# Fetching the features' operand pair by pair, with norm rows from short sends, in a linear-attention and expert kernel

## The reference

```python
def _phi(x, omega):
    m = omega.shape[1]
    proj = jnp.einsum('bhtd,dm->bhtm', x, omega)
    norm_sq_half = 0.5 * jnp.sum(x * x, axis=-1, keepdims=True)
    return jnp.exp(proj - norm_sq_half) / math.sqrt(m)
...
qkv = x @ W_attn + b_attn
q, k, v = jnp.split(qkv, 3, axis=-1)
...
phi_q = _phi(q, omega)
phi_k = _phi(k, omega)
kv = phi_k[..., :, None] * v[..., None, :]
S = jnp.cumsum(kv, axis=2)
Z = jnp.cumsum(phi_k, axis=2)
num = jnp.einsum('bhtm,bhtmd->bhtd', phi_q, S)
den = jnp.einsum('bhtm,bhtm->bht', phi_q, Z)[..., None] + EPS
y = num / den
...
h = _layernorm(x, axis=-1) * (1 + ca) + sa
x = x + ga * _L0_attn_ref(h, ...)
h = _layernorm(x, axis=-1) * (1 + cb) + sb
x = x + gb * _L0_ffn_ref(h, ...)
```

## Time and profile before

| | |
|---|---|
| time, median of 3 runs | 794.57 us (792.78 to 794.88) |
| the profiled execution | 791.14 us |
| its span, first to last instruction | 788.9 us |
| PE busy | 740.5 us, 94% |
| DVE, ACT, POOL busy | 526.3, 422.1, 62.7 us |
| DMA | 65.36 MB, 42804 packets, mean 83 GB/s |

### The profile page before, as it was taken

One profiled execution on the slowest core, in us unless ns is written; L12 is line 12 of the kernel. 1 busy time (PEld: TensorE's weight loads), 2 busy tenths in 40 slices (PEclk: granted clock), 3 DMA queues, 4 the chain that ended last, 5 costly groups with the idle time before them and its releaser, 6 DMA issues.

```text
span 788.9 us, 17005 instructions
## 1 busy us (share of the span) xinstructions
PE 740.5 (94%) x6138; PEld 605.5 (77%) x6138; DVE 526.3 (67%) x1265; ACT 422.1 (53%) x769; POOL 62.7 (8%) x72
## 2 busy tenths in 40 slices
PE   3889999999999999999999999999999999999696
PEld 3678768887698867887688876987678876987466
DVE  4366776676666776766776767767766767766456
ACT  3376636664556554665366745575456644564232
POOL 1260010001000010001000010000100010000100
PEclk9999999999999999999999999999999999999799
DMA  8750183103801065102811057010741029000000
GB/s 282 198 143 2 54 211 64 53 0 118 205 2 53 27 188 111 53 0 80 208 38 53 0 146 179 9 44 27 212 87 53 0 89 223 13 29 28 0 1 27
DMA packets 42804, 65.36 MB, mean 83 GB/s; under 512 B 5000, under 2 KB 19104, under 8 KB 42656
## 3 DMA queue, kind: packets, MB, share of 16 engines
q1 hardware_dynamic: 42784, 65.09, 30.6%
HBM read 39.91 MB, written 25.17 MB: 82 GB/s over the span
## 4 chain that ended last, share of the span: by engine, by line
PE 79%; DVE 12%; issue 3%; DMA 2%; ACT 2%; POOL 1%; DVEq 0%; SPq 0%; ACTq 0%; POOLq 0%
PE pa L579 11%; PE prod L592 7%; PE ring L428 6%; PE ring L558 5%; PE pa L428 5%; PE pa L430 5%; PE pa L429 5%; PE ring L430 4%; PE ring L429 4%; PE ring L612 4%; PE ring L563 3%; PE ring L720 2%; PE ring L619 2%; PE pa L693 2%; DVE am_phk L1178 2%
## 5 line engine op out<-in xcount | busy, mean ns | idle before, releaser
L579 PE MATMUL pa<-phq,phkT 128*128 128x128 f32 x768 | 101.2, 275 | 0.0
L1178 DVE TENSOR_TENSOR am_phk<-pa,const 128x512 f32<-128x512 f32 x112 | 77.0, 688 | 35.6 <-PE pa L579 34.6
L579 PEld LDWEIGHTS pa<-phq,phkT 128*128 128x128 f32 x768 | 95.4, 192 | 2.1
L1348 DVE SCALAR_TENSOR_TENSOR am_phk<-ring,am_phk 128x512 f32<-128x512 f32 x64 | 44.3, 691 | 53.2 <-PE ring L773 53.2
L988 ACT ACTIVATE qk_r<-phq 128x512 fp32r<-128x512 f32 x64 | 40.5, 633 | 63.7 <-DVE phq L1357 63.7
L428 PE MATMUL pa<-wo_r,qk_r 128*128 128x256 f32 x256 | 72.2, 282 | 0.6 <-DVE qk_l L1353 0.6
L430 PE MATMUL pa<-wo_l,qk_r 128*128 128x256 f32 x256 | 72.3, 282 | 0.0
L429 PE MATMUL pa<-wo_r,qk_l 128*128 128x256 f32 x256 | 72.0, 281 | 0.0
L558 PE MATMUL ring<-xq,omega_x 100*128 100x512 f32 x196 | 70.3, 440 | 1.4 <-DVE lora_w L1171 1.4
L918 ACT ACTIVATE phq<-ring 128x512 f32<-128x512 f32 x82 | 49.3, 602 | 36.1 <-PE ring L558 34.9
L918 ACT ACTIVATE phkT<-ring 128x512 f32<-128x512 f32 x98 | 58.3, 595 | 12.9 <-PE ring L558 12.6
(11 more groups left out here) (209 smaller groups left out, 1609.3 us busy)
## 6 DMA issues: line engine op xcount, KB each, us to landing
xq<-qk_parts SPq DMA_DIRECT2D x48, 512.0 KB
qk_parts<-qk_r SPq DMA_DIRECT2D x32, 256.0 KB, 4.4
qk_parts<-qk_l SPq DMA_DIRECT2D x32, 256.0 KB, 4.9
tok<-in_L_attn_x SPq DMA_DIRECT2D x8, 512.0 KB, 3.6
xr<-in_L_attn_x SPq DMA_DIRECT2D x8, 512.0 KB, 3.4
out_x<-tg SPq DMA_DIRECT2D x16, 256.0 KB, 2.2
norm_parts<-norm_r SPq DMA_DIRECT2D x16, 128.0 KB, 2.3
norm_parts<-norm_l SPq DMA_DIRECT2D x16, 128.0 KB, 2.4
```

The source lines that it names most:

```text
L579: mm = pe.matmul(score_bank(q, a)[:, tt], phkT[:, q % 2, a, tt], query(q)[:, a, tt], start=True, stop=True)
L1178: dve.tensor_tensor(am[:, 2 * (q % 2) + a, :].rearrange("p (c t) -> p c t", c=NT), score_bank(q, a)[:].rearrange("p (c t) -> p c t", c=NT) ...
L1348: dve.scalar_tensor_tensor(r2[:, f % 2, :], z_bank[f % 4][:], 0.0, rho, ALU.max, ALU.mult).then_inc(r2_done.sem, 1)
```

## The change

`xq` is laid out with the pair ahead of query/key, so that a pair's queries and keys lie side by side in a row; `qk_parts` is laid out so that each of its 128 rows holds the query tile and the key tile of a half next to each other (pieces of 4 KB instead of 2 KB for the fetch). Each half's norms are sent by four transfers of 8 rows instead of two of 64, into a layout from which one transfer of four rows fetches them. In block 0 the lead's pairs 0 and 1 are fetched alone, with a semaphore of their own (`lead_moved`); pairs 2 and 3 follow after the sends of half 1, and PE waits for them ahead of the features of pair 2.

```diff
-        xq = sb("xq", [XROWS, 2, 2, HALF, T], F32R)
+        xq = sb("xq", [XROWS, 2, HALF, 2, T], F32R)
...
-        norm_out = [sig(name, 2 * 16) for name in ("norm0_out", "norm1_out")]
-
-        moved = [sig(name, 5 * 16) for name in ("moved0", "moved1")]
+        norm_out = [sig(name, 4 * 16) for name in ("norm0_out", "norm1_out")]
+
+        moved = [sig(name, 4 * 16) for name in ("moved0", "moved1")]
+        lead_moved = sig("lead_moved")
...
+            def send(n, j):
+                wait(sp, qk_split, n, j + 1)
+                for part, src in enumerate((qk_r, qk_l)):
+                    sp.dma_start(parts_out[part, j // 2, :, j % 2], src[:, j, :].bitcast(F32)).then_inc(qk_out[j // 2].sem, 16)
+
+            def send_norms(n, half):
+                for part, src in enumerate((norm_r, norm_l)):
+                    for kind in range(2):
+                        row = (2 * half + kind) * VA
+                        sp.dma_start(norms_out[half, part, :, :, kind].rearrange("a i t -> (a i) t"),
+                                     src[row:row + 2 * GROUP, :].bitcast(F32)).then_inc(norm_out[half].sem, 16)
+
+            def fetch_qk(n, half, pairs, signal):
+                wait(sp, qk_out[half], n, qk_out[half].per)
+                for copy, part in enumerate((0, 0, 1)):
+                    src = parts_out[part, half].rearrange("(i r) k t -> r i (k t)", r=PAIR_ROWS)[:, pairs]
+                    sp.dma_start(xq[copy * PAIR_ROWS:(copy + 1) * PAIR_ROWS, half, pairs]
+                                 .rearrange("r i k t -> r i (k t)").bitcast(F32), src).then_inc(signal.sem, 16)
+
+            def fetch_norms(n, half, pairs, signal):
+                wait(sp, norm_out[half], n, norm_out[half].per)
+                src = norms_out[half, :, :, pairs].rearrange("q a i k t -> (q a) (i k t)")
+                sp.dma_start(xq[3 * PAIR_ROWS:XROWS, half, pairs].rearrange("r i k t -> r (i k t)").bitcast(F32),
+                             src).then_inc(signal.sem, 16)
+
+            first, second, both = slice(0, 2), slice(2, HALF), slice(0, HALF)
+
+            def first_front():
+                send(0, 0)
+                send(0, 1)
+                wait(sp, norm_split, 0, 1)
+                send_norms(0, 0)
+                fetch_qk(0, 0, first, lead_moved)
+                fetch_norms(0, 0, first, lead_moved)
+                send(0, 2)
+                send(0, 3)
+                wait(sp, norm_split, 0, 2)
+                send_norms(0, 1)
+                fetch_qk(0, 0, second, moved[0])
+                fetch_norms(0, 0, second, moved[0])
+                fetch_qk(0, 1, both, moved[1])
+                fetch_norms(0, 1, both, moved[1])
...
-                    if tile == 0:
+                    if tile == 0 and lead:
+                        pe.wait_ge(lead_moved.sem, 4 * 16)
+                    if tile == 0 and not lead:
                         wait(pe, moved[0], n, moved[0].per)
...
                 pe.wait_ge(late_vec.sem, 10)
+                pe.wait_ge(moved[0].sem, moved[0].per)
                 features(n, 2, first)
```

More of the change, by code:

```diff
@@ L330, in _ @@
             sp.sem_inc(scaled.sem, scaled.per)
[L332 to L356, removed]
@@ L358, in next_front @@
-            def next_front(n):
[L360 to L390, removed]
-                wait(sp, norm_split, n, 2)
[L392 to L396, removed]
@@ L398, in load_xr @@
+            def next_front(n):
+                send(n, 0)
+                send(n, 1)
+                fetch_qk(n, 0, both, moved[0])
+                send(n, 2)
+                send(n, 3)
+                wait(sp, norm_split, n, 2)
+                send_norms(n, 0)
+                send_norms(n, 1)
+                fetch_norms(n, 0, both, moved[0])
+                fetch_qk(n, 1, both, moved[1])
+                fetch_norms(n, 1, both, moved[1])
             def load_xr(n):
@@ L407, in ffn_stores @@
                                  tg[:, b, :].rearrange("p (t c) -> p t c", t=2)).then_inc(out_done.sem, 16)
-            front_moves(0)
+            first_front()
             sp.wait_ge(wp_done.sem, B)
@@ L557, in features @@
                     if k < 4:
-                        mm = pe.matmul(dst[:], omega_x[:, k // 2 * M:(k // 2 + 1) * M], xq[:, p // HALF, k % 2, p % HALF, :],
+                        mm = pe.matmul(dst[:], omega_x[:, k // 2 * M:(k // 2 + 1) * M], xq[:, p // HALF, p % HALF, k % 2, :],
                                        start=True, stop=True)
@@ L562, in features @@
                             t = (2 * (k - 4) + c) * P
-                            mm = pe.matmul(dst[:, c * 2 * M:(c + 1) * 2 * M], xq[:, p // HALF, 1, p % HALF, t:t + P], omega_x[:],
+                            mm = pe.matmul(dst[:, c * 2 * M:(c + 1) * 2 * M], xq[:, p // HALF, p % HALF, 1, t:t + P], omega_x[:],
                                            start=True, stop=True)
@@ L1548 @@
     out = nc.dram_tensor("out_x", (B, SEQ, C), F32, kind="ExternalOutput").ap()
-    parts_out = nc.dram_tensor("qk_parts", (2, 4, P, T), F32, kind="Internal").ap()
-    norms_out = nc.dram_tensor("norm_parts", (2, P, T), F32, kind="Internal").ap()
+    parts_out = nc.dram_tensor("qk_parts", (2, 2, P, 2, T), F32, kind="Internal").ap()
+    norms_out = nc.dram_tensor("norm_parts", (2, 2, 2, HALF, 2, T), F32, kind="Internal").ap()
     build(nc, *args, out, parts_out, norms_out)
```

## The result

The changed kernel took 786.51 us, the median of four runs (786.2 to 787.05), against 793.8 us for the kernel before in the same comparison. The ratio is 0.9917, 95% interval 0.9896 to 0.9939: 6.6 us faster by the ratio, between 4.8 and 8.3; the two medians lie 7.3 apart.

The account below looks back on a forecast made before the run. PE, busy 94% of the span, was taken as the bound, leaving only its own pauses to win. Lead -5.2 and loop +1.0 gave -4.2 us: 786.9 for the profiled execution, 790.4 on the median, range 787.4 to 794.0.

Parts of the forecast that it names:

- The place and the cause: Block 0, before the lead: PE's 4.05 us wait for norm rows behind 1.5 MB of queries and keys would go.
- only three large ones: Reading of PE's waits: 11.0 us for the first operand, 7.4 at the second layer norm, 4.0 for `xq<-norm_parts`.
- The 33.3 us: Block 0: time when the lead's bytes are through; from it pairs 2 and 3 were put at 43.3, needed at 49.05.
- The layout is worth nothing by itself: Fetch of `xq`: 4 KB pieces instead of 2 KB keep the rate of 206 GB/s; one norm transfer priced at nothing.
- The lead, -5.2 us: Block 0, lead to pair 2: exponentials start 4.2 us earlier and ACT's 1.01 us pause closes; pair 2 at 49.05.
- The loop, +1.0 us: Norm sends in the loop: eight at 0.40 us make the fetch 0.65 late; slack 0.5 leaves 0.15 in seven passes.
- So on the median I forecast 794.57 - 4.2: Whole kernel: the sum of -4.2 us, made on the profiled 791.14, carried to the median of the runs, giving 790.4.
- ACT's 1.01 us: Block 0, behind the lead's pause: ACT's second pause, laid to PE's half clock, expected to close.
- Rival 1 (dear short sends): Loop and lead: short sends cost 0.59 us like long ones; 801.1 us, slower; chance 0.1 to pass break-even.
- Rival 2 (four engines): Norm rows' transfer: four engines carry them twice as fast, 1.3 us earlier each pass, no loop loss; 789.4 us; chance 0.2.
- Rival 3 (the clock falls anyway): Block 0, weight splits: pause goes but PE's clock falls; 1.01 us stays, about 1 is added; 792.4 us; chance 0.15.
- Rival 4: Block 0: lead not ready in time, through half 1's sends or slower 4 KB pieces; 793 us; chance 0.1.

Follow-up runs that it names:

- the second profile of the kernel before: The kernel before rerun with no edit: 793.83 us, ratio 1.0003; its profiled execution has a span of 792.9 us at a mean clock of 0.984.
- The small loop: The kernel before plus 12 loop turns of a matmul nobody reads, between gates and lead, keeping PE busy while its operand is late: 790.15 us, ratio 0.9961.
- eight more sends: The changed kernel plus eight more 8-row sends in each loop pass, just ahead of the fetch of half 0's norm rows: 810.18 us.

## Why the prediction was right and wrong

- **The place and the cause** were right: the one wait for `xq<-norm_parts` is gone, half the bytes make the lead ready in time (6.7 us after issue against 7.2 computed), and nothing took the wait's place. The reading "only three large ones" passed over a row of 4.1 us in eight short pauses, which the change doesn't touch. The 33.3 us from which the moved transfers were counted isn't derived in the prediction; nothing hung on it, since PE waited for none of them.
- **The layout is worth nothing by itself** was right for the fetch, and the fetch alone in the old layout confirms it.
- **The lead, -5.2 us**: measured 5.7 between the two profiles, of which 0.16 is that the gates' copy came earlier (36.72 against 36.88). The chain through ACT and DVE was the right one. Against the second profile of the kernel before (pair 2 at 55.77) it is 7.2, of which 0.5 is that this execution ended its gates later.
- **The loop, +1.0 us, failed.** I took 0.40 us for an 8-row send and 0.5 us of slack. The runs show 0.295, and a slack of 1.0 in the changed kernel, which is 0.8 for the kernel before, whose fetch comes 0.19 us later behind its first send (2.90 against 2.71). Either alone would have made the term zero. Both errors had a cause in the way I read: an 8-row send lies below the 4-row load of 0.37, so the number of rows doesn't order these prices; and I shaved the slack below my own bounds of 0.6 to 1.1.
- **"So on the median I forecast 794.57 - 4.2" failed**, and this is the larger error. The sum was made against one execution that stood 3.4 us under the median of its runs, and I carried it over as if the missing time were a constant around it. It was half clock, and part of it stood right behind the pause that the change removes. The small loop prices the slow clock there: 3.1 us (1.7 to 4.4), where I had counted only ACT's 1.01 us. The way from the lead to pair 2 took 13.4 and 14.4 us in the two profiles of the kernel before and 14.2 with the lead's own fetch undone, and with a whole clock 12.0. With the pause of 4.1 us that gives 5.5 to 6.5 at the front, against 6.6 measured (4.8 to 8.3). The 3.9 us between forecast and median are then 1.0 from the loop's term, 0.5 from the lead's, 0.8 because the kernel before came out at 793.8 here and not at 794.57, and 1.6 left over. The added half clock at the front carries up to 1.0 of that; the remainder lies within the interval and can't be given to a place.
- **Rival 1 (dear short sends)** was the wrong way round: short sends are half as dear. But its size was under-priced too: at its full price each pass would have waited 1.65 us and lost its clock as well, as with eight more sends (24 us lost for 12 us of waiting).
- **Rival 2 (four engines)**: its time came nearest, 789.4, but by luck; the norm rows are at most 0.6 us faster, not 1.3, and the loop's loss is nothing for another reason. **Rival 3 (the clock falls anyway)** did not happen in the front; the last block has such stretches, in both kernels. **Rival 4** did not happen.
- **Open**: what decides whether the last block has one, two or three stretches at half clock. Its rows differ between executions of the same kernel, and no run here changed that block.

## What to carry to other kernels

When data is late at the start of a kernel, fetch first only what the first consumer reads; here the order of the fetches brought the whole 6.6 us within what can be measured, and larger pieces and fewer transfers brought nothing that can be told from zero. Price a pause of TensorE with the clock behind it, and look at the granted clock of the profiled execution before carrying its sum to the median: one that lies under its median may be the execution in which the clock fell least. An added wait on the engine that bounds the kernel is to be read in the same way: waits of 1.7 us a pass cost twice their length here, waits of 0.4 us did not.

## What was not expected of the hardware

- Pauses of PE of some 1.7 us in each pass of the loop were followed by stretches at 1.2 GHz (granted clock 0.50), which doubled their price; pauses of 0.4 us at the same place were not. In the run with 12 written-out matmuls the same followed five of six pauses of 1.9 to 2.3 us.
- Twelve matmuls written out ahead of the loop, which run once, made PE wait 2.1 us at the head of the loop in six passes, with 67 instruction packets (1.10 MB) instead of 13 (0.21 MB). Twelve turns of a small loop in the same place did not. The rows fit that part of the loop's code is loaded anew in each pass: 54 more packets of some 16 KB are nine in each of six passes. No run varied the loop's place or size by itself, so the mechanism is inferred. The Trainium skill ("Runtime: NRT & Kernel Launch", Instruction fetch mechanics) states such a mechanism: a taken branch to code that is not loaded waits for its fetch, and fetches come in blocks of 16 KiB; the size of these packets agrees.
- A send of 8 rows is issued in 0.295 us, one of 64 rows in 0.48 to 0.6 and one of 128 rows at the median in 0.33 (`qk_r`) or 0.43 (`qk_l`) on the same queue, so the price does not follow the number of rows.
